# Second feed-forward block's row statistics spread over the attention of later batches, and its first six chunks normed by GpSimd

## The reference, cut to what matters

```python
# x is (4, 1024, 128); FFN: 14 routed experts of which each row takes 2, and 2 shared experts, hidden 256
x = x + 0.5 * ffn(layernorm(x))
x = x + attention(layernorm(x))       # 16 heads of 8, causal, ALiBi
x = x + 0.5 * ffn(layernorm(x))

def ffn(x):
    gates = softmax(x @ router_w); top_v, top_i = top_k(gates, 2)
    masked = zeros.at[rows, top_i].set(top_v); masked /= masked.sum(-1) + 1e-9
    return sum_e masked[:, e] * expert(e, x) + sum_s expert(s, x)
def expert(e, x):
    h = x * rsqrt(mean(x * x) + 1.2e-7) * rms_w[e]
    return silu(h @ w1[e]) @ w2[e]
```

## Time and profile before

| | us |
|---|---|
| runs of the kernel before | 1133.79, 1138.70, 1140.87 (median 1138.7) |
| the profiled execution | 1135.14 |
| its span | 1133.4 |
| PE busy | 959.1 (85%) |
| DVE busy | 771.9 (68%) |
| ACT busy | 499.1 (44%) |
| POOL busy | 364.3 (32%) |

### The profile page before, as it was taken

One profiled execution on the slowest core, in us unless ns is written; L12 is line 12 of the kernel. 1 busy time (PEld: TensorE's weight loads), 2 busy tenths in 40 slices (PEclk: granted clock), 3 DMA queues, 4 the chain that ended last, 5 costly groups with the idle time before them and its releaser, 6 DMA issues.

```text
span 1133.4 us, 20376 instructions
## 1 busy us (share of the span) xinstructions
PE 959.1 (85%) x6961; PEld 577.0 (51%) x6961; DVE 771.9 (68%) x1855; ACT 499.1 (44%) x817; POOL 364.3 (32%) x415
## 2 busy tenths in 40 slices
PE   3675888878688999999999999998998885788994
PEld 3444788854224344443444444453334354778863
DVE  5873466747888678786787877878684365546654
ACT  1121454531134566545665556655456322444531
POOL 6665616453500220002200022000201456615464
PEclk9698899998769999999999999999799687989998
DMA  9612444454102132301324003240000003435522
GB/s 292 184 45 68 127 126 135 113 152 109 39 1 47 42 78 45 86 3 33 87 45 86 3 22 97 45 86 3 1 3 3 29 26 96 134 100 145 142 73 58
DMA packets 84252, 85.25 MB, mean 75 GB/s; under 512 B 11732, under 2 KB 73444, under 8 KB 81700
## 3 DMA queue, kind: packets, MB, share of 16 engines
q1 hardware_dynamic: 50950, 55.28, 18.5%
q0 software_dynamic: 8192, 16.79, 5.4%
q10 hardware_dynamic: 25024, 12.06, 3.6%
HBM read 52.48 MB, written 37.45 MB: 79 GB/s over the span
## 4 chain that ended last, share of the span: by engine, by line
PE 45%; issue 20%; DMA 16%; DVE 9%; POOL 3%; ACT 2%; another core or an unknown queue 2%; DVEq 1%; POOLq 1%; ACTq 0%; SPq 0%
PE banks L1685 10%; PE banks L1715 10%; DMA region_c<-sorted_y,pos 7%; PE banks L1698 7%; PE banks L1627 4%; DVE nmax L1301 4%; DMA region_b<-sorted_y,pos 3%; DMA region_a<-sorted_y,pos 3%; PE banks L1614 3%; PE banks L1688 2%; PE banks L1701 2%; DMA sorted_y<-ysb 1%; POOL region_c L739 1%; PE banks L1551 1%
## 5 line engine op out<-in xcount | busy, mean ns | idle before, releaser
L946 ACT ACTIVATE work<-banks 128x1024 f32<-128x1024 f32 (+3 forms) x384 | 301.2, 812 | 248.2 <-PE banks L1701 177.8
L1301 DVE TENSOR_REDUCE nmax<-banks 128x1 f32<-128x512 f32 (+3 forms) x432 | 275.3, 667 | 70.6 <-PE banks L1685 30.8
L1685 PE MATMUL banks<-ks,qs 75*128 75x512 bf16 (+3 forms) x576 | 183.9, 350 | 35.8 <-DVE nmax L1301 15.6
L1159 DVE SCALAR_TENSOR_TENSOR work<-work,banks 128x512 f32<-128x512 f32 x156 | 106.6, 685 | 102.1 <-ACT work L856 46.3
L1715 PE MATMUL banks<-work,vaug 128*9 128x512 f32 (+3 forms) x1536 | 167.1, 508 | 0.0
L1698 PE MATMUL banks<-qs,ks 78*128 78x512 bf16 (+3 forms) x576 | 159.8, 340 | 3.6 <-ACT work L946 3.6
L722 POOL DMA_INDIRECT sorted_x<-region_b,pos x128 | 127.6, 997 | 98.9 <-issue 32.3
L1301 DVE TENSOR_REDUCE nmax_late_keys<-banks 128x1 f32<-128x384 f32 (+3 forms) x176 | 111.4, 642 | 56.1 <-PE banks L1688 50.1
L1685 PEld LDWEIGHTS banks<-ks,qs 75*128 75x128 bf16 x576 | 56.6, 101 | 180.9 <-DVE nmax L1301 82.0
L1627 PE MATMUL banks<-region_c,work 128*128 128x128 f32 x736 | 105.4, 288 | 28.6 <-DVE work L1159 20.4
L1614 PE MATMUL banks<-xTp,region_c 128*128 128x128 f32 x736 | 103.6, 286 | 11.1 <-ACT xTp L850 9.8
(11 more groups left out here) (173 smaller groups left out, 1204.1 us busy)
## 6 DMA issues: line engine op xcount, KB each, us to landing
xld<-sorted_x SPq DMA_DIRECT2D x92, 128.0 KB
sorted_y<-ysb ACTq DMA_DIRECT2D x92, 128.0 KB
qs<-q_scr SPq DMA_DIRECT2D x36, 192.0 KB
ks<-k_scr SPq DMA_DIRECT2D x36, 192.0 KB
q_scr<-qp SPq DMA_DIRECT2D x20, 256.0 KB
k_scr<-kp SPq DMA_DIRECT2D x12, 256.0 KB
region_c<-q_scr SPq DMA_DIRECT2D x12, 192.0 KB
region_c<-k_scr SPq DMA_DIRECT2D x12, 192.0 KB
```

The source lines that it names most:

```text
L946: nc.scalar.activation(pT[s % 2][pair][:, :, 0:w], ps_s[pair][:, :, 0:w], ACT.Exp).then_inc(s_e, 1)
L1159: nc.vector.scalar_tensor_tensor(uu[slot], th[slot], 1.0, ps_h[slot], ALU.add, ALU.mult).then_inc(o.u, 1)
L1301: nc.vector.tensor_reduce(dst, ps_1[n % 2][:, 0:len(pieces) * w].rearrange("p (h j) -> p h j", j=w), axis=AXX, op=ALU.max, negate=True).th ...
L1685: last = mm(dst, qs[g][0:PASS1_ROWS, h, it * P:(it + 1) * P], ks[g][0:PASS1_ROWS, h, j0:j0 + w], start=True, stop=not diagonal)
```

## The change

- The attention's own norm gets its statistics in a new buffer `mva`, so that `mv` is free for the second block.
- DVE takes the second block's statistics of batch 0 during batch 1, and of batch 1 during batch 2, one tile at a time: after the reductions of s = 0, 4, 5, 6 of units g = 2 and 3. Those of batch 2 are taken in batch 3, g = 0, two tiles at each of s = 7, 8, 9, 10 (where the batches before take the next batch's own statistics).
- GpSimd norms chunks 0 to 5 (24 tiles) as soon as it is through with the last batch's values; DVE only chunks 6 and 7. Chunks 4 and 5 go to a free part of `region_a`.
- TensorE runs T4, T5, L4 and L5 after steps (3, 8), (3, 9) and (3, 10) instead of after the attention; T4 waits until group 0's rows are placed, whose ranks lie in the same bank.

```diff
-EARLY_HEAD = {(2, 9): "T0", (2, 10): "T1L0", (2, 11): "T2L1", (3, 0): "T3L2", (3, 1): "L3"}
+EARLY_HEAD = {(2, 9): "T0", (2, 10): "T1L0", (2, 11): "T2L1", (3, 0): "T3L2", (3, 1): "L3",
+              (3, 8): "T4", (3, 9): "T5L4", (3, 10): "L5"}
+ROWS_STATS_AT = [0, 4, 5, 6]
+POOLS_LATER_CHUNKS = range(6)
@@ GpSimd, ffn_norms
-                    if f or b != POOLS_BATCH:
+                    chunks = range(b * BT // CT, (b + 1) * BT // CT)
+                    if chunks[0] not in pools_chunks(f):
                         pool.drain().then_inc(o.rr, 1)
                         continue
-                    for c in range(b * BT // CT, (b + 1) * BT // CT):
+                    for c in chunks:
                         for t in range(c * CT, (c + 1) * CT):
-                            nc.gpsimd.tensor_scalar(xh_tile(t), xs[:, t, :], mv[:, t, 0:1], rr[:, t:t + 1],
+                            nc.gpsimd.tensor_scalar(xh_tile(f, t), xs[:, t, :], mv[:, t, 0:1], rr[:, t:t + 1],
                                                     ALU.subtract, ALU.mult)
                         pool.drain().then_inc(o.xh2, 1)
@@ ScalarE, run_ffn
-                for c in range(GC, CHUNKS):
-                    if f and c == GC + 2:
-                        for n in range(SHARED_FIRST):
-                            tanh(n)
+                if f:
+                    for n in range(SHARED_FIRST):
+                        tanh(n)
+                for c in range(GC + 2 if f else GC, CHUNKS):
                     transposed(f, c)
@@ VectorE, run_ffn
-                    chunk_normed(f, GC + 1)
@@ VectorE, steps
-                    if last and g == 1 and s == 0:
-                        batch_stats(1, 0)
-                        batch_stats(1, 1)
-                    if last and g == 2 and s < GC:
-                        if s == 0:
-                            dve.wait_ge(s_parts, 2 * BATCH)
-                            dve.wait_ge(s_va, BT * BATCH)
-                        chunk_normed(1, s)
-                    if last and g == 3 and s == 0:
-                        batch_stats(1, 2)
+                    if 0 < b < BATCH - 1 and g >= 2 and s in ROWS_STATS_AT:
+                        t = (b - 1) * BT + (g - 2) * BT // 2 + ROWS_STATS_AT.index(s)
+                        statistics(t, 1, t, mv)
+                        if (g, s) == (UNITS - 1, ROWS_STATS_AT[-1]):
+                            dve.drain().then_inc(ffn[1].mv, 1)
+                    if last and g == 0 and s in STATS_AT:
+                        t = (b - 1) * BT + STATS_AT.index(s) * NORM_TILES
+                        statistics(t, NORM_TILES, t, mv)
+                        if s == STATS_AT[-1]:
+                            dve.drain().then_inc(ffn[1].mv, 1)
@@ VectorE, after the last step
-                if name == "proj0":
-                    chunk_normed(1, GC)
@@ TensorE, run_ffn
-                if f:
-                    transposes(f, GC)
                 for n in range(2):
                     hidden(n, xT[n // NH])
                 if f:
-                    transposes(f, GC + 1)
-                    logits(f, GC)
-                    logits(f, GC + 1)
                     for n in range(SHARED_FIRST):
                         shared_unit(n)
@@ TensorE, steps
+                        if early == "T4":
+                            pe.wait_ge(ffn[1].pos, 1)
```

More of the change, by code:

```diff
@@ L303, in build, with xh_tile, pools_chunks @@
         xh = region_b.rearrange("p a (t d) -> p (a t) d", d=D)
-        def xh_tile(t):
+        def xh_tile(f, t):
+            if f and GT <= t < GT + BT:
+                return more_rows[:, t - GT, :]
             return xh[:, (t + GT) % TILES, :]
+        def pools_chunks(f):
+            return POOLS_LATER_CHUNKS if f else POOLS_CHUNKS
         got = [region.rearrange("p a (k t d) -> p (a k t) d", d=D, k=2).rearrange(
@@ L371, in ps_tr @@
                 return ps_r
-            return ps_t[1] if f and c < GC else ps_t[c % 2]
+            return ps_t[1] if f and c < GC + 2 else ps_t[c % 2]
         ps_tp = [banks[:, 2 + i, :] for i in range(2)]
@@ L997, in scale_weights, with statistics @@
                 dve.drain()
-            def statistics(t0, n, to):
+            def statistics(t0, n, to, means):
                 for t in range(n):
@@ L1003, in statistics @@
                 for t in range(n):
-                    nc.vector.bn_aggr(mv[:, to + t, :], stats[:, to % GT + t, :])
+                    nc.vector.bn_aggr(means[:, to + t, :], stats[:, to % GT + t, :])
             def batch_stats(f, b):
-                statistics(b * BT, BT, b * BT)
+                statistics(b * BT, BT, b * BT, mv)
                 dve.drain().then_inc(ffn[f].mv, 1)
@@ L1480, in transposes @@
                 o = ffn[f]
[L1481 to L1482 removed]
+                pools = pools_chunks(f)
+                if c in pools:
+                    pe.wait_ge(o.xh2, c - pools.start + 1)
                 else:
[L1484 removed]
+                    pe.wait_ge(o.xh, c + 1 if c < pools.start else c + 1 - len(pools))
                 if c >= (1 if f else 2):
[L1486 removed]
+                    pe.wait_ge(o.xts, c if f and c < GC + 2 else c - 1)
                 for t in range(CT):
                     last = nc.tensor.transpose(ps_tr(f, c)[:, t * P:(t + 1) * P],
[L1489 removed]
+                                               xh_tile(f, c * CT + t), ident[:, :])
                 last.then_inc(o.xt, 1)
```

23 lines of the change are left out of this document (10 added, 13 removed).

## The result

The changed kernel took 1148.88 us (median), the kernel before, in the same session, 1141.51 us: 7.4 us longer. The ratio is 1.0079, 95% interval 1.0048 to 1.0110. I had forecast -7.4 us and a range of 1124 to 1139 us; it came out 7 to 9 us longer, outside the range. By size it is still within the 1% that I named as the bound of what can be told.

What follows compares the result with a forecast made beforehand. It took TensorE, tied to DVE by two PSUM banks, to bound the attention, and GpSimd's chain the stretch behind. Terms -11.0 - 2.9 + 1.3 + 2.4 + 3.8 - 1.0 = -7.4 us gave 1138.7 - 7.4 = 1131.3 us, range 1124 to 1139.

Steps and rivals of the forecast that it cites:

- Term 1: Batch 3, g 1, s 0: statistics of batches 0 and 1 leave and the clock's fall goes with them; -11.0 us.
- term 2: Batch 3, g 2, s 0 to 3: DVE's chunk norms leave, GpSimd's norms instead are covered; -2.9 us.
- Term 3: Batch 3: batch 2's statistics leave g 3 at no gain and cost time in g 0, s 7 to 10; +1.3 us.
- Term 4: One-tile statistics in four units of batches 1 and 2 cost 0.6 us a unit; +2.4 us.
- Rival A: Batch 3, g 3: the clock also stays high at `ranks`, gaining 3.9 us more, time 1127.4 us; chance 0.15.
- Term 5: Last attention steps: T4, T5, L4 and L5 lengthen the chain of steps; +3.8 us, bounds 2.0 and 6.
- Term 6: Behind the attention: removed matmuls gain 0, within TensorE's 13.6 us slack; DVE's chunk 5 norm leaving GpSimd's powers gains -1.0 us.
- Term 7: Batch 3's attention: GpSimd's norms beside DVE's work delay at most the join of g 0; 0, bound +0.8 us.
- Rival E: 775 to 779 us: DVE's join and two parts each wait for a GpSimd norm; +2.4 us, 1133.7; chance within the forecast's 0.60.
- Rival B: Last attention steps: TensorE idles and its clock falls, +4 us, one-tile statistics +2, time 1137 us; chance 0.11.
- C: Batches 1 and 2: one-tile statistics make TensorE's clock fall in four units; +22.6 us, 1161; chance 0.04.
- D: Batch 3: the clock falls all the same, so the g 1 statistics gain only -4.7, time 1137.6 us; chance 0.07.

Runs made afterwards that it cites:

- a1: The changed kernel run again, unaltered; ratio 1.0000 to the kernel before on the same chip.
- c2: The changed kernel run again, unaltered, on another chip; ratio 1.0075 to the kernel before there.
- e1: The changed kernel run again, unaltered, on a further chip; ratio 1.0007 (medians) to the kernel before there.
- a3_tail_only: Against the changed kernel, statistics and norms of chunks 0 to 3 put back as before; T4 to L5 stay in the last steps; ratio 1.0146 to the kernel before.
- d3_L5_behind: The changed kernel with L5 alone moved behind the attention; ratio 1.0113 to the kernel before on the same chip.
- d1_scatter_later: The changed kernel with all 32 scatters of group 0 issued behind batch 3's powers; ratio 1.0114 to the kernel before on the same chip.
- c3: The changed kernel with T4, T5, L4 and L5 put back behind the attention; ratio 0.9945 to the kernel before on the same chip.
- e2: The changed kernel with T4, T5, L4 and L5 put back behind the attention, on a further chip; ratio 0.9951 to the kernel before there.
- b3: The changed kernel with L5 alone moved behind the attention, on the chip where the kernel before takes 1083.7 us; ratio 0.9922 to the kernel before.
- c4: The changed kernel with T4 to L5 moved ahead of `ranks`, where TensorE waits for `choose`; ratio 1.0003 to the kernel before on the same chip.
- d2: The changed kernel run again, unaltered, on another chip; ratio 1.0044 to the kernel before there.
- b1: The changed kernel with all scatters behind batch 3's powers, on the chip where the kernel before takes 1083.7 us; ratio 1.0055 to the kernel before.
- a4: The changed kernel with 16 unused transposes and logits' matmuls on TensorE while GpSimd makes powers; ratio 1.0033 to the kernel before.

## Why the prediction was wrong, point by point

- **Term 1 (-11.0) and term 2 (-2.9)** were right: the joins of batch 3 moved by -9.2 us (terms 1 and 3 together: -9.7) and -2.9 us.
- **Term 3 (+1.3)** was about 1.7, as 33.83 - 32.1 shows. **Term 4 (+2.4)** was right, 0.61 or 0.62 us in each of the four units; 0.35 us more stand in batch 2 between the joins of g 0 and g 1, which no term has.
- **Rival A** (0.15) came true as a mechanism: the clock was 1.00 at `ranks` in g 3. In a1, c2 and e1 it fell for 3.4 us, in before for 10. Why, no run shows; I had argued against it. With it the attention is short by 10.4 us, and the terms by 10.3.
- **Term 5 (+3.8)** is the first of the two steps that failed. Its size up to the last exponential was right with the clock high (steps of 3.19 and 3.50 us, forecast some 3), though with the tail alone the attention grew by 6.1 us in one trace (a3_tail_only). What I left out stands behind that: I priced L5 in front of the last weighing by TensorE's modelled durations, with 2.2 us from there to `o1` as before. It took 8.5 us. Moving L5 away took 7.0 us off (d3_L5_behind), keeping the scatters away 8.0 us (d1_scatter_later). That was an overlap that I took to be free: I had named the twelve scatters nowhere as a cost, since they use no resource of TensorE that the trace shows.
- **Term 6 (0)** is the second. The 0 us for the moved matmuls assumed that what TensorE, ACT or DVE do between the statistics and the first pair isn't on the path. In the changed kernel it is: `choose` of group 1 ended 9.4 us later behind `var_eps`, scatter 29 waited 4.34 us for it, and the first pair waited for DVE's last shared sum and not for its rows, 4.87 us where I had said over 13. That is the sign of being wrong that I had named, a head that doesn't hang on the scatters. Of the 9.9 us it takes 2.0, from scatter 13 to the first pair. The lateness is not that of the moved matmuls: `choose` is as late with the matmuls put back (c3, e2) and in time on the chip of b. The slack that I read from one wait of TensorE, 13.6 us, was that of another chain. The **-1.0 us** was wrong in its cause. I put GpSimd's gap down to DVE's norm of chunk 5 because they stood side by side, and named the rule of the Trainium skill (SBUF — State Buffer, "Who interferes with whom"), by which DVE in a two-port mode and GpSimd exclude each other, beside it. The norm went and the gap stayed, and another of 0.46 us came; the powers took 7.9 us instead of 7.5. The gap goes with scatters directly ahead. That agreement of row and rule was a coincidence of one trace.
- **Term 7 (0)**: the joins show nothing of it (0.17 us each). Rival E, DVE held up by the norms, did not occur there.
- **Rival B**: not in the changed kernel, but in the one trace of a3_tail_only, where the attention grew by 6.1 us instead of term 5's 3.8 (I had given the rival +4). **C**: no. **D**: no.
- **Where no release was late**, on the chip of b, the changed kernel with L5 moved (b3) has 0.9922, or -8.5 us, beside my -7.4 for the changed kernel. The terms of the attention hold; what was missing is what the late releases take back.
- **The start value.** I subtracted from 1138.7 us. The kernel before itself had medians of 1083.7 to 1158.8 us on five chips, and two identical kernels differ by 0.7% on one. A range of 15 us in absolute time was too narrow for that alone.

What stays open: why TensorE's completions are late beside the scatters, and on some chips only; none of the core's transfers of instructions (part 3 of the page, by their times) lies between 880.3 and 908.3 us in the changed kernel, so it isn't those. How the 12 scatters, L5 and the rest of the change share the loss isn't settled either, as d3 and c4 disagree. And of the 7 to 9 us by which the first comparison exceeds the kernel before, the stages up to the first pair account for none (-0.5 us): it lies in the pairs, if it is there at all, and no run tells it from the swing of that stretch. The changed kernel itself was not run on the chip of b, where its two variants gained 0.8 and 1.2%.

## What to carry to other kernels

A gain in front of a stretch counts only as far as the next handover: follow the chain past the end of the edit to the first thing that all work waits for, through every engine that feeds it, and ask which DMAs are being issued beside it. A slack read from one wait is the slack of the chain that ended it; a second chain can stand right behind it (here 5.2 us: the last shared sum of the kernel before ended that much ahead of the first pair). A single row next to a suspected cause is one coincidence; look for a second place where the effect stands without the cause before it becomes a term. For a change under 1%, run the kernel before as its own rival and on more than one chip.

## What the runs showed of the hardware

- Beside indirect DMAs of 128 rows, issued one in 1.26 us by GpSimd, releases by TensorE came up to 8.6 us later than the same ones without them (d1, d2), at equal clock. In fifteen traces 53 to 88 of TensorE's semaphore updates are over 0.5 us late, all within 5 us of such a DMA, and none of over 1,200 others. On one of the chips there was none of it in three kernels, and there the pairs ran in 96 to 97 us instead of 116 to 140, the kernel before in 1083.7 us.
- The same instruction of GpSimd started 1.15 us behind its predecessor with scatters ahead of it (16 traces) and 0.15 us behind it without (b1, d1).
- TensorE's modelled ends and the times of its weighings' semaphore agree within 0.1 us in the quiet case and are 6.6 (changed kernel) and 8.7 us (d2) apart for the last weighing in the disturbed one; an idle time whose releaser is "remote", on a kernel of one core, was the sign of it here.
- A filler of 16 matmuls and transposes right ahead of TensorE's wait did not keep its clock: 0.50 for 10.2 us with it (a4) and without it (a1).
